# A two-layer recurrent network on eight cores: expert weights loaded from another DMA queue, and a gated scan and a small FFN whose steps change engines

## The reference

```python
x = L0_attn_x                                  # 8 x 4096 x 1024
xn = _layernorm(x)
q, k, v = xn @ q_w, xn @ k_w, xn @ v_w         # 128 features each; M: 128 x 128 state
#   per token: retrieved = q M;  M = sigmoid(decay) * M + k v^T
s = retrieved @ o_w.T * out_scale
#   FFN 0: s_ = xn @ Win + bin (64); h = relu(s_[..., None] * W1 + b1) (64 x 16)
#          g = (h * W2).sum(-1) + b2;  out = g @ Wout + bout
x = x + s * _silu(FFN0(xn))
xn = _layernorm(x)
xi = xn @ W_in + b_in
gate_x, gate_a = sigmoid(xi @ W_gx + b_gx), sigmoid(xi @ W_ga + b_ga)
log_a = -8.0 * gate_a * softplus(a_param)
a, scale = exp(log_a), sqrt(1.0 - exp(2.0 * log_a))
#   per token: h = a * h + scale * gate_x * xi
s = h @ W_out + b_out
#   FFN 1: 8 experts (1024 -> 4096 -> 1024, gelu), every expert on every token,
#          the one with the largest gate logit kept by a one-hot mask
x = x + s * _silu(FFN1(xn))
```

## Time and profile before

| | us |
|---|---|
| runs: median, lowest, highest of 7 | 10368.16, 10161.21, 10484.16 |
| the profiled execution: its own time | 10163.88 |
| its span (core 2, the slowest), all cores | 10162.8, 10130.8 to 10162.8 |
| busy: PE, weight loads, DVE, ACT, POOL | 8328.2, 3610.3, 1736.8, 2027.9, 1845.4 |

### The profile page before, as it was taken

The page is one execution under the profiler, slowest core; times in us unless marked ns, Lnnn a source line. Parts: engine busy times, 40 slices in busy tenths (PEclk is TensorE's granted clock), DMA queues, the critical chain, the costliest instruction groups (busy, mean ns, idle before and its releaser), DMA issues.

```text
span 10162.8 us, 103726 instructions; the slowest of 8 cores (10130.8 to 10162.8 us)
## 1 busy us (share of the span) xinstructions
PE 8328.2 (82%) x36733; PEld 3610.3 (36%) x36733; DVE 1736.8 (17%) x2818; ACT 2027.9 (20%) x3381; POOL 1845.4 (18%) x3268
## 2 busy tenths in 40 slices
...
GB/s 140 176 183 180 181 184 186 187 169 200 196 202 196 205 162 112 71 112 100 96 107 92 110 125 143 90 109 80 108 81 106 95 109 83 112 71 112 94 132 119
DMA packets 361096, 1350.36 MB, mean 133 GB/s; under 512 B 54854, under 2 KB 129096, under 8 KB 282766
## 3 DMA queue, kind: packets, MB, share of 16 engines
...
...
## 4 chain that ended last, share of the span: by engine, by line
PE 72%; DMA 12%; DVE 7%; issue 3%; ACT 3%; ACTq 1%; DVEq 0%; POOL 0%; SPq 0%; POOLq 0%
PE p2pb L1068 33%; PE p2pb L1080 31%; DMA w2sb<-w2bfT 4%; DMA s2tA<-s2scr 2%; DMA w1tB<-w1bfT 2%; DMA s2scr<-tp 2%; ACT pb L245 2%; PE pb L862 1%; PE pb L615 1%; PE pb L612 1%; ACTq L149 1%; PE pb L878 1%; DVE tp L930 1%; DVE tp L639 1%; PE pb L688 0%
## 5 line engine op out<-in xcount | busy, mean ns | idle before, releaser
L1080 PE MATMUL p2pb<-hfm,w2sb 128*128 128x512 bf16 x16384 | 3546.5, 379 | 39.1 <-ACT hfm L245 39.1
L245 ACT ACTIVATE hfm<-p2pb 128x512 bf16<-128x512 f32 x2048 | 1222.7, 597 | 6037.7 <-PE p2pb L1068 4771.1
L1080 PEld LDWEIGHTS p2pb<-hfm,w2sb 128*128 128x128 bf16 x16384 | 1598.5, 98 | 1974.6 <-issue 56.4
L1068 PE MATMUL p2pb<-xnm,w1tA 128*128 128x512 bf16 x8192 | 1860.0, 386 | 484.1 <-ACT hfm L245 473.9
L1068 PE MATMUL p2pb<-xnm,w1tB 128*128 128x512 bf16 x8192 | 1828.1, 382 | 66.4 <-DMA w1tB<-w1bfT 65.9
L1068 PEld LDWEIGHTS p2pb<-xnm,w1tA 128*128 128x128 bf16 x8192 | 810.2, 99 | 1493.2 <-issue 562.0
L1068 PEld LDWEIGHTS p2pb<-xnm,w1tB 128*128 128x128 bf16 x8192 | 803.8, 98 | 1053.8 <-issue 106.5
L1046 DVE TENSOR_TENSOR xnm<-xn1s,p2pb 128x512 bf16<-128x512 bf16 x512 | 351.9, 687 | 4098.9 <-PE p2pb L1041 3995.8
L108 POOL CAST cstgb<-cstgf 128x512 bf16<-128x512 f32 x1088 | 677.0, 622 | 495.1 <-DMA cstgf<-L_ffn_W 459.7
L212 POOL DMA_DIRECT2D cstgf<-L_ffn_W x1024 | 551.3, 538 | 22.3 <-issue 18.6
L212 POOL DMA_DIRECT2D w1bfT<-cstgb x512 | 279.3, 546 | 662.8 <-DMA w1bfT<-cstgb 556.3
(11 more groups left out here) (227 smaller groups left out, 3049.7 us busy)
## 6 DMA issues: line engine op xcount, KB each, us to landing
cstgf<-L_ffn_W POOLq DMA_DIRECT2D x1024, 256.0 KB, 3.4
w1tA<-w1bfT ACTq DMA_DIRECT2D x256, 1024.0 KB, 4.8
w1tB<-w1bfT ACTq DMA_DIRECT2D x256, 1024.0 KB, 4.9
w2sb<-w2bfT ACTq DMA_DIRECT2D x64, 2048.0 KB, 8.9
w1bfT<-cstgb POOLq DMA_DIRECT2D x512, 128.0 KB, 2.0
w2bfT<-cstgb POOLq DMA_DIRECT2D x512, 128.0 KB, 2.0
xn1s<-xn1scr SPq DMA_DIRECT2D x64, 1024.0 KB, 6.2
xa<-xT SPq DMA_DIRECT2D x8, 2048.0 KB, 17.1
```

The source lines that it names most:

```text
L245: return self.op("se", lambda e: e.activation(out, in_, fn_func, bias=bias, scale=scale), reads=reads, writes=writes)
L1068: p.op("pe", lambda e, hc=hc, hs=hs, ic=ic, pb=pb, wt=wt: e.matmul(pb[0][:, :], wt[:, ic * HC + hs * 128: ic * HC + (hs + 1) * 128], xnm[: ...
L1080: p.op("pe", lambda e, dc=dc, ht=ht, pb=pb: e.matmul(pb[0][:, :], w2sb[:, ht * D + dc * 128: ht * D + (dc + 1) * 128], h_fm[:, ht * 512:(h ...
```

## The change

It has five parts. (1) `emit_w2load` issues on SP's queue, and each quarter of `w2sb` has a `Buf` of its own, for which the matmuls wait by quarter. (2) The output DMAs of the last expert go to SP's queue, and the writes to `out` and to `s2scr` are tracked by four `Buf`s in turn. (3) The scan loop is split: first sixteen exps (into `s0` and eight `tp` tiles), then per block ACT relu(1 - e) into one tile `rstage`, ACT sqrt into `ga_all`, DVE times `xg_all`, DVE scan back into `ga_all`, DVE copy to `hcar`, DVE cast to `h_bf`. (4) In FFN 0 the relu leaves ACT: DVE does multiply-add, max with 0, and the accumulation in one chain. (5) `tp` has 8 tiles instead of 6. `emit_qkv` becomes a list of pieces that is run at the same place.

```diff
+                _AF.Gelu: "gelu", _AF.Tanh: "gelu", _AF.Silu: "silu",
+                _AF.Sqrt: "sqrt"}
...
+    s2w = [Buf() for _ in range(4)]
...
-    tp = [p.S(f"tp{i}", [128, TC], F32) for i in range(6)]
+    tp = [p.S(f"tp{i}", [128, TC], F32) for i in range(8)]
+    rstage, rstage_b = p.S("rstage", [128, TC], F32)
...
         for h in range(INNER):
-            rp = PBt[2 + h % 2]
-            par = h % 2
-            k = h // 2
-            ga_o, ga_ob = gaccs[(k % 2) * 2 + par]
-            ga_i, ga_ib = gaccs[((k + 1) % 2) * 2 + par]
-            p.act(AF.Relu, rp[0][0:MF, :], sF[:, :], bias=b1c[:, h:h + 1], scale=w1c[:, h:h + 1],
-                  reads=(sF_b, b1c_b, w1c_b), writes=(rp[1],))
-            if h < 2:
-                p.op("ve", lambda e, h=h, rp=rp, ga_o=ga_o: e.tensor_scalar_mul(ga_o[:, :], rp[0][0:MF, :],
-                                                                                w2c[:, h:h + 1]),
-                     reads=(rp[1], w2c_b), writes=(ga_ob,))
+            t1 = TP()
+            p.op("ve", lambda e, h=h, t1=t1: e.tensor_scalar(
+                t1[0][0:MF, :], sF[:, :], w1c[:, h:h + 1], b1c[:, h:h + 1], OP.mult, OP.add),
+                 reads=(sF_b, w1c_b, b1c_b), writes=(t1[1],))
+            t2 = TP()
+            p.op("ve", lambda e, t1=t1, t2=t2: e.tensor_scalar_max(t2[0][0:MF, :], t1[0][0:MF, :], 0.0),
+                 reads=(t1[1],), writes=(t2[1],))
+            ga_o, ga_ob = gaccs[h % 2]
+            ga_i, ga_ib = gaccs[(h + 1) % 2]
+            if h == 0:
+                p.op("ve", lambda e, t2=t2, ga_o=ga_o: e.tensor_scalar_mul(ga_o[:, :], t2[0][0:MF, :],
+                                                                           w2c[:, 0:1]),
+                     reads=(t2[1], w2c_b), writes=(ga_ob,))
             else:
-                p.op("ve", lambda e, h=h, rp=rp, ga_o=ga_o, ga_i=ga_i: e.scalar_tensor_tensor(
-                    ga_o[:, :], rp[0][0:MF, :], w2c[:, h:h + 1], ga_i[:, :], OP.mult, OP.add),
-                     reads=(rp[1], w2c_b, ga_ib), writes=(ga_ob,))
+                p.op("ve", lambda e, h=h, t2=t2, ga_o=ga_o, ga_i=ga_i: e.scalar_tensor_tensor(
+                    ga_o[:, :], t2[0][0:MF, :], w2c[:, h:h + 1], ga_i[:, :], OP.mult, OP.add),
+                     reads=(t2[1], w2c_b, ga_ib), writes=(ga_ob,))
...
-        p.op("ve", lambda e: e.tensor_tensor(gfin[:, :], geven[:, :], godd[:, :], OP.add),
-             reads=(geven_b, godd_b), writes=(gfin_b,))
+        gfin, gfin_b = gaccs[(INNER - 1) % 2]
...
-            ap_ = PBt[2 + oc2 % 2]
-            p.act(AF.Exp, ap_[0][:, :], ga_all[:, osl], reads=(ga_all_b,), writes=(ap_[1],))
-            e2a = TP()
-            e2b = TP()
-            p.act(AF.Exp, PSm[:, :], ga_all[:, osl], scale=2.0, reads=(ga_all_b,), writes=(PSm_b,))
-            p.op("ve", lambda e, e2a=e2a: e.tensor_scalar(e2a[0][:, :], PSm[:, :], -1.0, 1.0, OP.mult, OP.add),
-                 reads=(PSm_b,), writes=(e2a[1],))
-            p.op("ve", lambda e, e2a=e2a, e2b=e2b: e.tensor_scalar_max(e2b[0][:, :], e2a[0][:, :], 1e-38),
-                 reads=(e2a[1],), writes=(e2b[1],))
-            lnt = TP()
-            p.act(AF.Ln, lnt[0][:, :], e2b[0][:, :], reads=(e2b[1],), writes=(lnt[1],))
-            p.act(AF.Exp, PSm[:, :], lnt[0][:, :], scale=0.5, reads=(lnt[1],), writes=(PSm_b,))
-            p.op("ve", lambda e, osl=osl: e.tensor_tensor(ga_all[:, osl], PSm[:, :],
-                                                          xg_all[:, osl], OP.mult),
-                 reads=(PSm_b, xg_all_b), writes=(ga_all_b,))
-            hf = TP()
-            p.op("ve", lambda e, osl=osl, hf=hf, ap_=ap_, oc2=oc2: e.tensor_tensor_scan(
-                hf[0][:, :], ap_[0][:, :], ga_all[:, osl],
+            p.act(AF.Exp, s0[:, osl], ga_all[:, osl], reads=(ga_all_b,), writes=(s0_b,))
+            p.act(AF.Exp, tp[oc2][0][:, :], ga_all[:, osl], scale=2.0,
+                  reads=(ga_all_b,), writes=(tp[oc2][1],))
+        for oc2 in range(FC):
+            osl = slice(oc2 * TC, (oc2 + 1) * TC)
+            p.act(AF.Relu, rstage[:, :], tp[oc2][0][:, :], bias=1.0, scale=-1.0,
+                  reads=(tp[oc2][1],), writes=(rstage_b,))
+            p.act(AF.Sqrt, ga_all[:, osl], rstage[:, :], reads=(rstage_b,), writes=(ga_all_b,))
+            p.op("ve", lambda e, osl=osl, oc2=oc2: e.tensor_tensor(tp[oc2][0][:, :], ga_all[:, osl],
+                                                                   xg_all[:, osl], OP.mult),
+                 reads=(ga_all_b, xg_all_b), writes=(tp[oc2][1],))
+            p.op("ve", lambda e, osl=osl, oc2=oc2: e.tensor_tensor_scan(
+                ga_all[:, osl], s0[:, osl], tp[oc2][0][:, :],
                 hcar[:, oc2:oc2 + 1], OP.mult, OP.add),
-                reads=(ap_[1], ga_all_b, hcar_b), writes=(hf[1],))
-            p.op("ve", lambda e, oc2=oc2, hf=hf: e.tensor_copy(hcar[:, oc2:oc2 + 1], hf[0][:, TC - 1:TC]),
-                 reads=(hf[1],), writes=(hcar_b,))
-            p.op("se", lambda e, oc2=oc2, hf=hf: e.copy(h_bf[:, oc2 * TC:(oc2 + 1) * TC], hf[0][:, :]),
-                 reads=(hf[1],), writes=(h_bf_b,))
+                reads=(s0_b, tp[oc2][1], hcar_b), writes=(ga_all_b,))
+            p.op("ve", lambda e, oc2=oc2: e.tensor_copy(hcar[:, oc2:oc2 + 1],
+                                                        ga_all[:, oc2 * TC + TC - 1:oc2 * TC + TC]),
+                 reads=(ga_all_b,), writes=(hcar_b,))
+            p.op("ve", lambda e, oc2=oc2, osl=osl: e.tensor_copy(h_bf[:, osl], ga_all[:, osl]),
+                 reads=(ga_all_b,), writes=(h_bf_b,))
...
-        if c + 1 < NCH and STAGE >= 99:
-            emit_qkv()
+        for u in qunits:
+            u()
...
             p.dma("se", s2ap[oc2 * 128:(oc2 + 1) * 128, c * TC:(c + 1) * TC], s2t[0][:, :],
-                  reads=(s2t[1],), writes=(s2scr_b,))
+                  reads=(s2t[1],), writes=(s2w[oc2 % 4],))
...
+    w2qb = [Buf() for _ in range(4)]
...
+    outw = [Buf() for _ in range(4)]
...
     def emit_w2load(e_):
         for qq in range(4):
-            p.dma("se", w2sb[:, qq * 8 * D:(qq + 1) * 8 * D],
+            p.dma("sy", w2sb[:, qq * 8 * D:(qq + 1) * 8 * D],
                   w2bf[e_, :, qq * 8 * D:(qq + 1) * 8 * D],
-                  reads=(w2bufs[e_],), writes=(w2sb_b,))
+                  reads=(w2bufs[e_],), writes=(w2qb[qq],))
...
-                    reads=(w2sb_b, h_fm_b), writes=(pb[1],))
+                    reads=(w2qb[ht // 8], h_fm_b), writes=(pb[1],))
...
-                p.dma("se", out[dc * 128:(dc + 1) * 128, tsl], c0[0][:, :],
-                      reads=(c0[1],), writes=(out_b,))
+                p.dma("sy", out[dc * 128:(dc + 1) * 128, tsl], c0[0][:, :],
+                      reads=(c0[1],), writes=(outw[dc % 4],))
```

49 lines of the change are left out of this document (28 added, 21 removed).

## The result

| | before | after |
|---|---|---|
| runs: median, lowest, highest | 10298.46, 10160.21, 10484.16 (31) | 9865.18, 9687.54, 9922.83 (12) |
| the profiled execution, its own time | 10163.88 | 9690.28 |
| start of unit 0's second part, median core | 2461.3 | 2311.4 |

The changed kernel is faster: the ratio is 0.9511, interval 0.9462 to 0.956 (that of the two medians is 0.958).

What follows compares the result with a forecast made beforehand. Waits between a chunk's steps bound the attention stage, PE and its pauses the expert stage. 10,164 - 150 (attention) - 441 (experts) = 9,573 us; a quarter of the 2.0% spread gave a median of 9,620, range 9,390 to 9,900.

Steps and rivals of the forecast that it cites:

- Scan loop: Attention stage: exps run early, each block a ring through ACT and DVE at 3.7 us; -188 us in eight chunks.
- W_out: Attention stage, W_out to sF: four Bufs let PE set the pace, 25.1 to 16.1 us a chunk; -72 us.
- FFN 0: Attention stage, sF to gbf: DVE does three operations a hidden unit, 18.3 to 32.1 us a chunk; +110 us.
- 1.95 a unit: FFN 0: DVE time for one hidden unit, multiply-add 0.64, max 0.59 and accumulation 0.72 us, sixteen a chunk.
- Expert switches: Expert stage: waits for hfm and w1tB and slow starts go, -608 us; W1 beside W2 costs 7 at 16 switches, +112.
- A stall of 3.7, the fourth about 2 more: Expert switch: PE waits 3.7 us for the third W1 piece, sharing with W2, about 2 for the fourth.
- that a piece takes beyond its bytes: Expert switch: 2 us added to a W1 piece's 8.7 us of transfer at a third of the bandwidth.
- I take 7 of 12.2: Last expert's six units: 7 us of each 12.2 us pause stays, +42 us; bounds 0 and 14.
- Rival B: Expert switches: W1 gets nothing until W2 is through, +254 us, 9,827 us; chance 0.17.
- C: Expert stage: no pause left at switches or in the last expert's units, 9,419 us, low end 9,387; chance 0.13.
- D: Expert stage: moving the loads brings nothing, only the attention stage gains, 10,014 us; chance 0.07.
- E: Expert stage: dense PE work lowers its granted clock; slower than before below 0.923, 12,062 us at 0.74; chance 0.05.

Runs made afterwards that it cites:

- b4_ga_tiles: Changed kernel with a Buf for each of ga_all's eight feature tiles in the scan loop; scans 2.76 us apart, unit 0's second part 60 to 71 us earlier on four cores.
- b3_s2_one: Changed kernel with DMAs to s2scr tracked by one Buf again; W_out to sF 25.7 to 27.3 us over all cores, against 15.7 to 15.9.
- a1_w2_act: Changed kernel with W2 loads back on ACT's queue, quarter Bufs kept; 17 us a switch, 7,456 to 7,492 us from unit 0's second part, against 7,328 to 7,370.
- a4_w2_between: Changed kernel with W2 in eighths behind W1's pieces on ACT's queue; 0 to 1 us a quiet switch, 7,202 to 7,218 us from unit 0's second part (four cores).
- b1_out_pool: Changed kernel with the last expert's output DMAs on POOL's queue; six units' extra time 51 us against 69, median tile 8.0 us against 8.4.

## Why the prediction was right, and where it was not

The median, 9,865, lies within the range and 245 us above the forecast; the profiled execution's 9,690 lies 117 above the sum of 9,573 that was made for it. The direction and the mechanisms were those of the forecast. Of the 245 us, 117 lie in the kernel's work and 128 in the step from one execution to the median.

**Scan loop: right.** A block takes 3.69 us (forecast 3.7), and PE's wait for `qT` fell in seven chunks from 336.4 to 168.2 us in all, 24.0 each (24.8). b4_ga_tiles shows the ring to be the one named.

**W_out: right, in part by luck.** 15.9 us to `sF` (16.1), and the wait is the one named (b3_s2_one). But "8 x 9.0" counts eight steps from W_out to `sF` where there are seven, and takes one chunk's 25.1 us for all: over the seven, core 2 took 179.4 us before, the last alone 33.0, and core 1 of the changed kernel 111.3. The gain is 68, at 9.7 a step (72 forecast), because the two errors nearly cancel.

**FFN 0: right in kind, too small.** 34.4 us instead of 32.1, +129 instead of +110. The step that failed is "1.95 a unit": it prices three passes by rows of DVE alone and has no term for POOL's casts, which run beside the chain. The two new DVE operations average 664 and 492 ns, the accumulation 801:

```profile
L754 DVE SCALAR_TENSOR_TENSOR gacc<-tp,w2c,gacc 64x512 f32<-64x512 f32 x120 | 96.1, 801 | 12.8 <-DVE tp L745 0.5
L741 DVE TENSOR_SCALAR tp<-sF,w1c,b1c 64x512 f32<-64x512 f32 x128 | 85.0, 664 | 160.0 <-ACTq L151 160.0
L745 DVE TENSOR_SCALAR tp<-tp 64x512 f32<-64x512 f32 x128 | 62.9, 492 | 18.8 <-DVE tp L741 4.9 <-DMA s2scr<-tp 3.2
```

Single ones stretch. The max of two hidden units on DVE:

```profile
1263.90 0.42 DVE L745 TENSOR_SCALAR tp<-tp 64x512 f32<-64x512 f32 x1
...
1267.83 1.07 DVE L745 TENSOR_SCALAR tp<-tp 64x512 f32<-64x512 f32 x1
```

POOL at the second of them:

```profile
1267.98 0.62 POOL L110 CAST cstgb<-cstgf 128x512 bf16<-128x512 f32 x1
```

The max that takes 0.42 us took 1.07 while POOL's cast ran from 1267.98 to 1268.60. Over the eight chunks of core 1 the maxes average 0.43 us without a cast beside them and 0.61 with one, the multiply-adds 0.54 and 0.80, the accumulations 0.74 and 0.88. Before, the accumulation read one operand from PSUM and took 0.74 us with a cast beside it or without (55 and 57 of 112, core 2). On core 1 the excess sums to 31 of the 129 us; the only two hidden units that have no cast beside them took 1.83 and 1.90 us, where the mean of all is 2.11. So without the casts 1.95 would have been about right. No run was made without the casts. The Trainium skill, "SBUF — State Buffer", section "SBUF: two separate sides", says that DVE and GpSimd share one pair of ports, and that a GpSimd instruction, or a DVE operation in a 2-port mode or with two SBUF inputs, holds it for the whole instruction while the other waits. The trace agrees in the length: the max took 0.65 us longer, and the cast 0.62.

The three terms with FFN 0 as measured give -188 - 72 + 129 = -131 (with W_out's 68 it is -127); the last W_out matmul ends 130.9 us earlier (median core, 2344.2 to 2213.3).

**Expert switches: the right mechanism, a mis-sized stall.** The wait for `hfm` is gone there, and a1_w2_act and a4_w2_between show W1's place against W2 to be the rest. "A stall of 3.7, the fourth about 2 more" was 5.5 on the third piece and none on the fourth, since that one had 14.6 us to land in 12.3. The failed step is the 2 us "that a piece takes beyond its bytes": while the engines are full the first packet of the third piece moves only 3.8 us after its issue (8276.80). With a slow start of 2.4 instead of 1.5 a quiet switch costs 8 (forecast 7), 10 to 11 where two neighbours' loads meet, for which the sum had no term. The first three, with POOL's casts still moving data, cost 10 to 17. Fifteen switches came to 166, with the one behind the last expert, against 115.

**Last expert: the path right, the size wrong.** "I take 7 of 12.2" was 11.5 (69 / 6), 27 us more in all. Moving the store took ACT's wait away and slowed the loads behind it on SP by nearly as much: with the store on POOL's queue the six units cost 51, not 69.

**The switch behind the last expert's first half** was put at 17 and took 18 to 31; the reason given, W2 behind the stores on SP, was not what PE waited for: it waited for `hfm` and W1, in the changed kernel and in b1_out_pool, and never for `w2sb`.

The attention stage (19 us), the switches (51) and these six units (27) make 97 of the 117 us between the sum and the profiled execution, on the median core.

**From the sum to the median.** "A quarter of the 2.0%" was too little: the new median lies 1.8% above its profiled execution (the old one, over 31 runs, 1.3%).

Rival B's time, 9,827, is near the median by chance, since its mechanism does not hold: W1 does advance beside W2. C and D fall with the waits above. E's drop does not show in the whole units above, where PEclk is 1.00.
